# A hint for the branch back of the first hop's loop, on all five engines

## The reference, cut to what matters

```python
# x: (100000, 256) f32; src, dst: (25000,), dst sorted; edge_weight: (25000,)
# shared_weight: (1024, 256); output_bias: (256,)
def _spmm(edge_src, edge_dst, edge_weight, feats, n_nodes):
    msgs = edge_weight[:, None] * feats[edge_src]
    return jax.ops.segment_sum(msgs, edge_dst, num_segments=n_nodes)
feats = [x]; cur = x
for _ in range(n_blocks - 1):              # n_blocks = 4: three hops
    cur = _spmm(edge_src, edge_dst, edge_weight, cur, n_nodes)
    feats.append(cur)
concat = jnp.concatenate(feats, axis=1)
out = _layernorm(x + concat @ shared_weight + output_bias)
```

## Time and profile before

| | |
|---|---|
| median of 3 runs | 1740.88 us |
| the profiled execution | 1738.98 us, span 1737.0 us |
| TensorE busy | 1582.6 us, 91% of the span |
| VectorE, ScalarE, GpSimd busy | 68%, 66%, 61% |
| granted TensorE clock, mean | 0.967 |
| DMA, mean | 260 GB/s |

### The profile page before, as it was taken

How to read it: one execution, slowest core, us unless ns; L and a number is a source line. 1 busy time by engine, 2 the same in 40 slices (tenths; PEclk the granted TensorE clock), 3 DMA queues, 4 the chain that set the end, 5 groups by cost and what they waited for, 6 DMA issues and landing times.

```text
span 1737.0 us, 37008 instructions
## 1 busy us (share of the span) xinstructions
PE 1582.6 (91%) x8468; PEld 1346.1 (77%) x8468; DVE 1174.0 (68%) x4883; ACT 1148.5 (66%) x3038; POOL 1064.9 (61%) x1044
## 2 busy tenths in 40 slices
PE   6899898988989899986986999969999999999993
PEld 5688787877878688875875888858888888888882
DVE  6767576766757577996763455527777777777773
ACT  3687676766767675664774565626777777777774
POOL 2277575756657571255776555555777777777764
PEclk9999999999999999998998999989999999999996
DMA  7599797978879897665896788767888888888862
GB/s 257 173 346 333 270 329 264 327 271 313 285 275 325 274 325 255 240 213 179 310 341 233 191 214 208 203 162 236 274 274 275 276 273 270 278 276 276 271 206 90
DMA packets 217741, 451.23 MB, mean 260 GB/s; under 512 B 30445, under 2 KB 125994, under 8 KB 217623
## 3 DMA queue, kind: packets, MB, share of 16 engines
q1 hardware_dynamic: 167730, 343.20, 56.7%
q0 software_dynamic: 49456, 106.58, 21.7%
q10 hardware_dynamic: 436, 0.20, 0.0%
HBM read 232.78 MB, written 225.74 MB: 264 GB/s over the span
## 4 chain that ended last, share of the span: by engine, by line
PE 71%; DVE 10%; issue 8%; DMA 5%; POOL 3%; ACT 1%; DVEq 1%; POOLq 0%; SPq 0%; ACTq 0%
PE ps_y L1218 30%; PE ps_xT L1209 7%; PE ps_u L1284 7%; PE ps_sum L1251 5%; PE ps_sum L1423 5%; PE ps_u L1423 5%; PE ps_u L1278 2%; PE ps_list L1384 2%; PE ps_u L1384 2%; DVE stats L1498 2%; DVE y_ring L1492 2%; POOL rows_in L707 2%; DMA rows_in<-in_x,gather_idx 1%; DMA c_rows<-sums,scatter_idx 1%; PE ps_u L1417 1%
## 5 line engine op out<-in xcount | busy, mean ns | idle before, releaser
L1218 PE MATMUL ps_y<-w_sb,xT 128*128 128x256 f32 x3128 | 814.2, 387 | 15.9 <-DVE y_ring L1492 15.9
L1218 PEld LDWEIGHTS ps_y<-w_sb,xT 128*128 128x128 f32 x3128 | 569.8, 194 | 79.7 <-issue 16.0
L1492 DVE TENSOR_TENSOR y_ring<-ps_y,bias 128x512 f32<-128x512 f32 x391 | 269.8, 690 | 255.6 <-PE ps_y L1218 255.2
L943 ACT ACTIVATE o_ring<-y_ring,shift,rstd 128x256 f32<-128x256 f32 (+1 forms) x782 | 421.7, 590 | 0.0
L930 ACT COPY xT<-ps_xT 128x512 f32<-128x512 f32 x391 | 227.6, 582 | 204.0 <-PE ps_xT L1209 195.9
L707 POOL DMA_INDIRECT tails_found<-tail_keys,table_idx x200 | 200.8, 1004 | 183.5 <-issue 51.9
L1498 DVE BATCH_NORM_STATS2 stats<-y_ring 128x6 f32<-128x256 f32 (+1 forms) x782 | 290.9, 414 | 4.8
L1209 PE MATMUL ps_xT<-ident,x_ring 128*128 128x128 f32 x1564 | 240.8, 277 | 23.2 <-ACT xT L930 14.3
L707 POOL DMA_INDIRECT rows_in<-in_x,gather_idx x200 | 200.8, 1004 | 81.9 <-issue 68.6
L711 POOL DMA_INDIRECT out_rows<-u_out,tailo_idx x197 | 197.8, 1004 | 85.3 <-issue 39.3
L707 POOL DMA_INDIRECT rows_in<-in_x,tailx_idx x197 | 202.2, 1027 | 77.5 <-issue 46.1
(11 more groups left out here) (231 smaller groups left out, 2141.5 us busy)
## 6 DMA issues: line engine op xcount, KB each, us to landing
x_ring<-in_x SPq DMA_DIRECT2D x195, 512.0 KB, 6.1
out_rows<-o_ring SPq DMA_DIRECT2D x195, 512.0 KB, 4.1
c_rows<-zeros SPq DMA_DIRECT2D x50, 512.0 KB
c_rows<-sums SPq DMA_DIRECT2D x50, 512.0 KB
u_rows<-u_out SPq DMA_DIRECT2D x50, 512.0 KB, 8.5
keys_bc<-keys_out SPq DMA_DIRECT2D x64, 256.0 KB, 3.6
keys_bc<-u_rows SPq DMA_DIRECT2D x25, 512.0 KB, 5.6
tails_found<-u_rows SPq DMA_DIRECT2D x12, 512.0 KB
```

Source lines behind the costliest of these rows:

```text
L943: last = act.activation(o_ring[slot][0:rows, r * D:(r + 1) * D], y_ring[k][0:rows, r * D:(r + 1) * D], ACT.Identity, bias=shift[k][0:rows, ...
L1218: last = pe.matmul(ps_y[bank][0:rows, r * D:(r + 1) * D], xT[bank][:, q * P:q * P + rows], w_sb[:, c, :], start=c == 0, stop=c == KC - 1)
L1492: dve.tensor_tensor(y_ring[k][0:rows, half * 2 * D:(half + 1) * 2 * D], ps_y[half][0:rows, :], bias2[0:rows, :], ALU.add).then_inc(y_copie ...
```

## The change

```diff
@@ -406,7 +406,7 @@
 
             for a in range(A_FIRST):
                 run(a, a_step(a), a % 3)
-            with eng.Fori(0, A_TURNS) as h:
+            with nc.Fori(0, A_TURNS, engines=[eng.engine], hint_back_edge=True) as h:
                 for i in range(A_TURN):
                     run(A_TURN * h + A_FIRST + i, a_step(A_FIRST + i, h), i)
             for a in range(A_LAST, A_STEPS):
```

## The result

The changed kernel takes 1701.98 us (median of 4 runs, 1701.6 to 1704.5) against 1740.86 us for the kernel before (4 runs): ratio 0.9781, 95% interval 0.9769 to 0.9794. The forecast was 1699.0, in a range of 1693 to 1724. The profiled execution took 1701.6 us, with a span of 1699.8.

The account below looks back on a forecast made before the run. TensorE, busy 91% of the span, was taken to pace the kernel, idling at VectorE's branch stalls. 6 x (7.59 - 0.40 - 0.20) = 41.9 us off the median 1740.88 gave 1699.0, range 1693 to 1724.

Parts of the forecast that it names:

- The place: First hop's loop: the 5.9 us idle before VectorE's index staging is its branch waiting for code, not a gather.
- The removed stall: VectorE's loop branch: the 7.59 us lost at each of six branches shrink to 0.40.
- The clock: TensorE behind the branch: no long idling, so no lower clock, and the next step's extra 2.31 us go.
- The next piece: VectorE's code after the loop's head: fetched 0.2 us late each turn, bounds 0 and 1.2.
- its turn is a little longer than what its code memory keeps: VectorE's loop: the reason given for the head's code being displaced by the time the branch wants it.
- five transfers a turn: Instruction queue in the loop: about five code transfers a turn stay, since the hint brings code earlier without sparing it.
- The other engines' hints: The four engines besides VectorE: their code is there already, so their hints cost nothing, 0.6 us if uncovered.
- slower: Rival, chance 0.07: the hint makes ScalarE stall 5.2 us at its loop branch each turn; 1786 us if VectorE's stall stays.
- partly: Rival, chance 0.12: VectorE's stall moves one piece on, half of the 7.59 us is kept, 1718 us.
- nothing: Rival, chance 0.13: the hint is not acted on, or too early, and each turn costs the same, 1741 us.
- The DMA: First hop's loop: data keeps up with faster turns at 327 GB/s, costing nothing; 4 us if gathers came late.

Follow-up runs that it names:

- e1: The changed kernel with the hint on VectorE's loop alone: 1699.02 us, ratio 0.9764 to the kernel before.
- e2: The changed kernel with hints on the four other engines and none on VectorE: 1743.89 us, ratio 1.0018 to the kernel before.
- e6: Hint on VectorE alone, its turn 42 memsets longer, head at slot 0 (four pieces): ratio 0.9914 to the kernel before on the same slower chip.
- e3: The changed kernel with hints on all engines but ScalarE: 1700.18 us, ratio 0.9769 to the kernel before.
- e9: The kernel before with the first hop's and last stage's steps written out, no loops: 1931.41 us, ratio 0.9642 on the same slower chip.
- e7: Hint on VectorE alone, ScalarE's unhinted loop head moved to slot 111 (four pieces): 1977.36 us, ratio 0.9831 to the kernel before on the same slower chip.
- e5: Hint on VectorE alone, its turn 42 memsets longer, head at slot 100 (five pieces): ratio 0.9957 to the kernel before on the same slower chip.
- e10: The changed kernel with the hint on the last stage's loop too: 1969.56 us, ratio 0.9816 to the kernel before on the same slower chip.

## Why the prediction was right, point by point

The place was right: the 5.9 us that the profile put down to a gather were VectorE's branch. e1 and e2 show it: the hint on that engine alone gives everything, on the four others nothing.

The removed stall: forecast 7.59 less 0.40 for a branch that finds its code. Measured 7.18, so 0.41; the row of the last stage was a good neighbour. The clock came back with it, as forecast.

The next piece, late by 0.20 us: wrong, it is never late, since nothing is fetched in the loop. The step that failed is "its turn is a little longer than what its code memory keeps". The turn fits, as even one of 430 instructions does when it lies in four pieces (e6: 3 transfers), and what lacked room was the fetch past the branch. The forecast that five transfers a turn would remain fell with it. It cost only 1.2 us in the sum, because a row bounded it: 6 x 7.18 = 43.1 instead of 41.9. The number came right although the reason for the missing code was wrong: what a branch costs with and without its code was taken from rows, and these hold whatever displaced the head.

The other engines' hints, costed at nothing: ScalarE's costs 3.1 us at one place behind the loop, in the change's trace. It accounts for most of what the median lies above the forecast: 1699.0 - 1.2 + 3.1 = 1700.9, measured 1701.98. The two misses pull opposite ways, and that they partly cancel is luck. The rival "slower" had the right engine and the wrong place. That ScalarE's code comes late there because the hint held back the fetch past the branch fits the three transfers seen, but no run isolates it. The rivals "partly" and "nothing" fell with the trace: the branch takes 0.3 us, and no step is longer than 22.5 us but the one with the branch (22.8 to 23.0).

The profile's gain, 37.2, is less than 43.2 - 3.1 = 40.1. Behind the pause the traces of e1, e3 and the change lose another 1.9 to 2.8 us on the kernel before, in the second hop; e2 loses 2.6 there too, without any gain in stage A. So it doesn't look like the change's doing: the profiled execution of before, 1.9 us under its median, seems to have been the quick one there.

The DMA: 327 GB/s forecast, 330 measured over 400 to 475, and no late gathers in the loop.

## What to carry to other kernels

Look at the sequencer's own rows (branch to next instruction) on every engine before believing a releaser in front of a loop's first instruction: a branch that finds its code takes 0.2 to 0.4 us, one that doesn't 5 to 6.5. Put the hint only on an engine that shows the gap; on the others it bought nothing, and ScalarE's made a pause behind the loop that cost 1.2 us in one trace and 3.1 in another. Where code size allows, write the loop out: here that was worth another 15 us over the best hinted kernel. Most of it is paid in each step, by register work in front of the instructions that TensorE waits for, and not at the branch.

## What the runs showed of the hardware

VectorE and ScalarE fetch code in pieces of 8 KB, and the runs fit with four held. A turn in three pieces runs without a hint, in four only with one (ScalarE: 5.1 to 6.5 us a branch without it, 0.2 with it), in five it makes 32 transfers of code in some six turns even with a hint.

A piece is about 128 instructions. In e9, where nearly all code runs once, the four engines other than TensorE execute 14223 instructions and bring 110 pieces, 129 each; TensorE executes 18392 and brings 72 pieces of 16 KB, 255 each.

Where the head of a loop falls in a piece can decide that: the head at slot 111 gave ScalarE six stalls (e7), where its branches took 0.2 to 0.3 us with the head unmoved (e5, e6).

The Trainium skill, in Runtime: NRT & Kernel Launch, section Instruction fetch mechanics, has 512 instructions in two blocks of 256, fetched purely in sequence, for an engine like these. The total agrees with four pieces of 128. The size of a block does not (8 KB a transfer here), nor does the sequence: with a hint the head comes out of turn, and VectorE goes on 0.5 to 2.4 us behind the branch where five pieces had displaced it.

Two other chips ran the kernel before in 2007 and 2008 us instead of 1740. In the trace of e10 packets took as long (queue q1: 167730 packets in 50.7% of 16 engines' 1968.4 us, 95 ns each, against 94 ns in the kernel before), but came with more idle time between them. The cause stays open. The change's mechanism shows there too, but six stalls of 6 us on ScalarE made no difference in time that the runs could show.
